# Silu as one activation for both gates of a selective-scan mixer, two elementwise steps moved from VectorE to GpSimd, and a new order of calls

## The reference, cut to what matters

```
# block 1: gated linear recurrence
x_conv = causal_depthwise_conv(x, conv_weight, conv_bias)            # 4 taps
r = sigmoid(x_conv @ Wr.T + Wr_b);  i = sigmoid(x_conv @ Wi.T + Wi_b)
a = sigmoid(log_a) ** (8 * r)
b = sqrt(clip(1 - a * a, 1e-6)) * (i * x_conv)
log_A = clip(cumsum(log(clip(a, 1e-7))), -80)                         # the limit of the decays
h = exp(log_A) * cumsum(b * exp(-log_A))
x = layernorm(x + rmsnorm(h @ out_w.T) * norm_w)
# block 2: x = layernorm(x + relu(x @ W1 + b1) @ W2 + b2)
# block 3: the mixer, with N = 16 states a channel
x_in, z = split(x @ in_proj_w.T)
x_c = silu(causal_depthwise_conv(x_in))                               # gate 1
B, C, dt = split(x_c @ x_proj_w.T);  dt = softplus(dt * dt_w + dt_b)
for t: h = exp(dt*A) * h + dt * B * x_c;  y = sum_n h * C
x = layernorm(x + (y * silu(z)) @ out_proj_w.T)                       # gate 2, the read-out of y
# block 4: x = layernorm(x + relu(x @ w1 + b1) @ w2 + b2)
```

## Time and profile before

| | |
|---|---|
| median of 3 runs | 961.75 us (959.28 to 962.03) |
| profiled execution | 961.2 us, its span 959.4 us |
| mean granted TensorE clock | 0.916 |
| busy PE / DVE / ACT / POOL | 796.9 / 802.2 / 671.6 / 561.4 us |
| instructions in the trace | 9608 |

### The profile page before, as it was taken

How to read it: one execution, slowest core, us unless ns; L and a number is a source line. 1 busy time by engine, 2 the same in 40 slices (tenths; PEclk the granted TensorE clock), 3 DMA queues, 4 the chain that set the end, 5 groups by cost and what they waited for, 6 DMA issues and landing times. The chain is left out here.

```text
span 959.4 us, 9608 instructions
## 1 busy us (share of the span) xinstructions
PE 796.9 (83%) x2802; PEld 528.2 (55%) x2802; DVE 802.2 (84%) x1013; ACT 671.6 (70%) x1345; POOL 561.4 (59%) x468
## 2 busy tenths in 40 slices
PE   2385867978987799999899999998998797787585
PEld 1264644736554556475647564756476546546464
DVE  5245566677799999999999999999999999989761
ACT  4347687588767865997699769876976685465452
POOL 0202457437836793789378937893776376565421
PEclk9597977989998889999999999999999799789597
DMA  9000000000100010001000100010000000000000
GB/s 315 12 23 22 23 1 22 1 1 0 56 1 0 1 42 13 0 1 59 8 1 1 60 1 0 1 46 0 1 1 27 1 1 1 23 0 1 22 1 22
DMA packets 10341, 19.49 MB, mean 20 GB/s; under 512 B 1457, under 2 KB 5297, under 8 KB 10289
## 3 DMA queue, kind: packets, MB, share of 16 engines
q1 hardware_dynamic: 10288, 18.88, 5.8%
HBM read 14.69 MB, written 4.19 MB: 20 GB/s over the span
## 5 line engine op out<-in xcount | busy, mean ns | idle before, releaser
L385 POOL TENSOR_TENSOR y<-y,hC 128x1024 f32<-128x1024 f32 (+3 forms) x140 | 280.1, 2001 | 77.3 <-DVE hC L1461 73.4
L1914 PE MATMUL pC<-w,hT 128*128 128x256 f32 x1024 | 232.4, 382 | 4.9 <-ACT hT L754 4.9
L819 ACT ACTIVATE dA<-dt,A_neg 128x512 f32<-128x512 f32 (+3 forms) x320 | 187.5, 630 | 54.3 <-DVE hs L1450 53.8
L1914 PEld LDWEIGHTS pC<-w,hT 128*128 128x128 f32 x1024 | 194.5, 191 | 36.7 <-issue 7.2
L1450 DVE TENSOR_TENSOR_SCAN hs<-dA,carry,pS 128x512 f32<-128x512 f32 (+3 forms) x192 | 193.4, 1008 | 18.1 <-ACT dA L819 10.4
L2037 PE MATMUL pS<-stack,sel 97*128 97x512 f32 (+3 forms) x320 | 148.0, 515 | 54.5 <-DVE hs L1450 54.0
L1435 DVE TENSOR_TENSOR pS<-u,pS 128x1024 f32<-128x1024 f32 (+3 forms) x160 | 159.8, 999 | 17.4 <-PE pS L2037 16.8
L1461 DVE TENSOR_TENSOR hC<-hs,pS 128x1024 f32<-128x1024 f32 (+3 forms) x160 | 157.5, 985 | 15.3 <-PE pS L2037 15.1
L1450 DVE TENSOR_TENSOR_SCAN hs<-dA,pS 128x512 f32<-128x512 f32 (+1 forms) x128 | 138.2, 1080 | 14.6 <-POOL carry L392 6.0
L754 ACT ACTIVATE hT<-pA,ffb_sb 128x512 f32<-128x512 f32 (+3 forms) x160 | 94.7, 599 | 59.2 <-PE pA L1907 58.9
L1907 PE MATMUL pA<-tg,w 128*128 128x512 f32 (+3 forms) x320 | 127.9, 538 | 7.7 <-ACT hT L754 6.3
(11 more groups left out here) (120 smaller groups left out, 1101.5 us busy)
## 6 DMA issues: line engine op xcount, KB each, us to landing
xt<-xT SPq DMA_DIRECT2D x6, 515.0 KB, 4.7
xtok<-x SPq DMA_DIRECT2D x6, 512.0 KB, 5.3
out<-x3b SPq DMA_DIRECT2D x6, 512.0 KB, 2.9
w<-w1a SPq DMA_DIRECT2D x1, 1024.0 KB, 8.3
w<-w2a SPq DMA_DIRECT2D x1, 1024.0 KB, 10.4
w<-w1b SPq DMA_DIRECT2D x1, 1024.0 KB, 8.3
w<-w2b SPq DMA_DIRECT2D x1, 1024.0 KB, 9.9
xt<-xT SPq DMA_DIRECT2D x2, 259.0 KB, 7.8
```

What stands on the lines that cost most here:

```text
L385: nc.gpsimd.tensor_tensor(y[:, :, 0:ch.T], so_far, hC[:, n % CRING, :, 0:ch.T], ALU.add).then_inc(S["y_sum"], 1)
L819: nc.scalar.activation(dA[:, k % ARING, 0:ch.T], dt[ch.side][:, h, 0:ch.T], ACT.Exp, scale=A_neg[:, h, n:n + 1]).then_inc(S["dA_ready"], 1)
L1914: mm = nc.tensor.matmul(dst[:, b * D:b * D + D], src(k, t0), w[:, k, :], start=k == 0, stop=k == nk - 1)
```

## The change

Both gates become one Silu activation on ScalarE; the VectorE halves and all factors 0.5 go. `decay_steps` and `readout` become GpSimd instructions. `z_silu` now waits for the read-out of the chunk two before, whose buffer it writes. Then all calls of all engines are put into another order in `opening`, `entry`, `step` and `closing`.

```
# ScalarE
-            def z_tanh(ch, h):
-                act.wait_ge(S["z_mm"], H * ch.i + h + 1)
-                nc.scalar.activation(zz[ch.side][:, h, 0:ch.T], pC[h][:, 0:ch.T], ACT.Tanh, scale=0.5).then_inc(S["tz_ready"], 1)
+            def z_silu(ch, h):
+                if ch.i > 1:
+                    act.wait_ge(S["yg_ready"], ch.i - 1)
+                act.wait_ge(S["z_mm"], H * ch.i + h + 1)
+                nc.scalar.activation(zz[ch.side][:, h, 0:ch.T], pC[h][:, 0:ch.T], ACT.Silu).then_inc(S["zz_ready"], 1)
-            def mconv_tanh(ch):
+            def mconv_silu(ch):
...
-                nc.scalar.activation(v[:, :, 0:ch.T], cv[:, :, 0:ch.T], ACT.Tanh, scale=0.5).then_inc(S["tcv_ready"], 1)
+                nc.scalar.activation(v[:, :, 0:ch.T], cv[:, :, 0:ch.T], ACT.Silu).then_inc(S["v_ready"], 1)
-                nc.scalar.mul(stack[ch.side][0:NXK, 0:ch.T], pA[0][0:NXK, 0:ch.T], 0.5).then_inc(S["stack_hi"], 1)
+                nc.scalar.copy(stack[ch.side][0:NXK, 0:ch.T], pA[0][0:NXK, 0:ch.T]).then_inc(S["stack_hi"], 1)
# VectorE
-            def z_silu(ch, h):
-                dve.wait_ge(S["tz_ready"], 2 * ch.i + h + 1)
-                V.scalar_tensor_tensor(out=zz[ch.side][:, h, 0:ch.T], in0=zz[ch.side][:, h, 0:ch.T], scalar=1.0, in1=pC[h][:, 0:ch.T],
-                                       op0=ALU.add, op1=ALU.mult).then_inc(S["zz_ready"], 1)
-            def mconv_silu(ch):
-                dve.wait_ge(S["tcv_ready"], ch.i + 1)
-                V.scalar_tensor_tensor(out=v[:, :, 0:ch.T], in0=v[:, :, 0:ch.T], scalar=1.0, in1=cv[:, :, 0:ch.T], op0=ALU.add,
-                                       op1=ALU.mult).then_inc(S["v_ready"], 1)
-                V.scalar_tensor_tensor(out=u[:, :, 0:ch.T], in0=dt[ch.side][:, :, 0:ch.T], scalar=0.5, in1=v[:, :, 0:ch.T], op0=ALU.mult,
-                                       op1=ALU.mult).then_inc(S["u_ready"], 1)
+                V.tensor_tensor(u[:, :, 0:ch.T], dt[ch.side][:, :, 0:ch.T], v[:, :, 0:ch.T], ALU.mult).then_inc(S["u_ready"], 1)
# from VectorE (dve.) to GpSimd (pool.)
+            def decay_steps(ch):
+                c = ch.i
+                pool.wait_ge(S["la_scan"], 2 * c + 2)
+                nc.gpsimd.tensor_tensor(decay[:, :, 0:ch.T], st[:, 0:H, 1:1 + ch.T], st[:, 0:H, 0:ch.T], ALU.subtract).then_inc(S["dl_ready"], 1)
+            def readout(ch, gate):
+                if gate is not None:
+                    conv_done(pool, gate)
+                pool.wait_ge(S["y_sum"], ADDS * (ch.i + 1))
+                nc.gpsimd.tensor_tensor(yg[:, :, 0:ch.T], y[:, :, 0:ch.T], zz[ch.side][:, :, 0:ch.T], ALU.mult).then_inc(S["yg_ready"], 1)
# GpSimd, one place of the new order in step()
                 if tail is not None:
                     sum_states(tail, NS - 1)
+                    readout(tail, gate)
```

More of the change, by code:

```diff
@@ L431, in entry @@
                         save_carry(scan, 1)
+                if gate is not None:
+                    decay_steps(gate)
+                if scan is not None:
+                    if scan.i > 0:
                         sum_states(scan, 1)
@@ L440, in entry @@
                         sum_states(scan, 3)
+                if prep is not None:
+                    mconv_add(prep, 1)
+                if scan is not None:
                     sum_states(scan, 4)
@@ L828, in opening @@
                     log_decay(gate)
+                if prep is not None:
+                    normalize(LN_PREP, prep, x2[prep.side])
+                if gate is not None:
                     gate_tanh(gate, 1, 0)
@@ new lines, in entry @@
+                if scan is not None:
+                    state_decay(scan, 12)
+                    state_decay(scan, 13)
+                if gate is not None:
+                    relu(0, gate, 1)
+                    relu(0, gate, 2)
+                if ahead is not None:
+                    conv_tap(ahead, 2, prep)
+                if tail is not None:
+                    row_squares(LN_OUT, tail, x3b, x3)
+                if gate is not None:
+                    relu(0, gate, 3)
+                    relu(0, gate, 4)
@@ new lines, in entry @@
+                if scan is not None:
+                    state_decay(scan, 14)
+                if gate is not None:
+                    relu(0, gate, 5)
+                if scan is not None:
+                    state_decay(scan, 15)
+                if tail is not None:
+                    normalize(LN_OUT, tail, x3b)
+                if gate is not None:
+                    relu(0, gate, 6)
+                    relu(0, gate, 7)
+                if ahead is not None:
+                    conv_tap(ahead, 3, prep)
@@ L894, in entry, with step @@
+            def step(ahead, gate, prep, scan, tail):
                 if tail is not None:
@@ L1121, in step @@
                     state_decay(scan, 12)
+                if prep is not None:
+                    step_sizes(prep)
+                if ahead is not None:
+                    conv_first(ahead)
                 if gate is not None:
@@ L1133, in step @@
                 if gate is not None:
-                    relu(0, gate, 1)
                     relu(0, gate, 2)
-                    relu(0, gate, 3)
-                if scan is not None:
-                    state_decay(scan, 15)
+                if ahead is not None:
+                    conv_tap(ahead, 2, prep)
                 if tail is not None:
@@ L1651, in entry @@
                     state_input(scan, 15)
-                if prep is not None:
-                    dt_x(prep)
-                if scan is not None:
                     state_scan(scan, 15, 0)
@@ L1669, in step @@
                     state_input(scan, 1)
+                if prep is not None:
+                    add_ffn0(prep, 0, tail)
+                if scan is not None:
                     state_scan(scan, 1, 0)
@@ L1743, in step @@
                     state_output(scan, 8)
-                if prep is not None:
-                    x_proj_low(prep)
-                if scan is not None:
                     state_scan(scan, 9, 1)
@@ L2256, in step @@
                     gate_mm(gate, 0, 1)
-                    gate_mm(gate, 1, 0)
+                if scan is not None:
+                    spread_B(scan, 3)
                 if tail is not None:
```

943 lines of the change are left out of this document (445 added, 498 removed).

## The result

The changed kernel takes 1001.5 us (median of 4 runs, 1000.8 to 1002.9), the kernel before 960.5 us beside it: a ratio of 1.043, with a 95% interval of [1.040, 1.045]. The forecast was 948.5 us.

What follows compares the result with a forecast made beforehand. VectorE was taken to bound the full steps, TensorE close behind. Gains in five stretches, less losses at start and end, summed to -12.8 us from 961.2, 948.4, left at 948.5; 8-in-10 range 934 to 965.

Steps and rivals of the forecast that it cites:

- The lengths that were kept: VectorE in a full step: four instruction groups go, 4.6 us less work, with other instructions as long as before.
- 2.5 us gained in each full step: Three full steps: each falls from 95.4 to 92.9 us, the middle of 90.9 and 95.4; -7.5 us in all.
- The step ahead of them: Stretch from 275.0 to 373.3 us: VectorE loses 4.1 us, TensorE has 14.5 to spare; taken as -3 us.
- the frame of 90.9 to 95.4: Full step length: 90.9 us if TensorE's waits are all absorbed, 95.4 if none are.
- The loads: ScalarE: 43 table loads become 80, 1.38 us each, 5.5 us a full step, 51 us in all; still below VectorE's work.
- The row that I called exp: ScalarE: a 1024-element activation of 1.06 us, used with tanh to price Silu as no change, up to 0.3 us a step.
- GpSimd's own time: GpSimd: two added steps a chunk, 4.9 us, make 73.6 us in a full step; busy near 600 us overall.
- The price that I gave, 1.2 us if the cover is gone: Results waiting behind GpSimd's moved steps: none counted in full steps, 1.2 us each if other work no longer covers them.
- The slower one, at 976 us: Rival: ScalarE sets the pace, its waits staying on top of 83.2 us of work; 0.16 together with the drain rival.

Runs made afterwards that it cites:

- e12: The changed kernel with gate input, scaled input, recurrence and u on VectorE cut to 8 columns: 962.6 us, 1.001 of the kernel before.
- e13: The kernel before with gate input, scaled input, recurrence and u on VectorE cut to 8 columns: 954.0 us, ratio 0.992.
- e8: The kernel before, old order of calls, with all helper edits but Tanh in place of each Silu, so no added loads: 953.7 us, ratio 0.992.
- e7: The changed kernel with a Tanh in place of each Silu, so no added loads: 1001.9 us against 1001.5 with them.
- e15: The changed kernel with the same four VectorE kinds cut to 8 columns and Tanh in place of each Silu: 960.1 us, 0.998 of the kernel before.
- e1: The kernel before, in its old order of calls, with only the two gates made Silu activations on ScalarE: 990.2 us, ratio 1.030.

## Why the prediction was wrong

- **The lengths that were kept.** The sum took 4.6 us a full step off VectorE and left the length of every other instruction as it was. This step failed, and it carries the most: in the full step after, recurrence, u, gate input and clip take 8.1 us more, and over the span these four groups take 42 us more. The price of it in time is about 31 of the 41 us, if the cut work of e12 and e13 is worth the same in both; how the 8.7 us that stay between e12 and e13 divide between the hold that the cut left and the new order's own chain is open. I had read the new order for loads and queues, not for what stands on GpSimd beside VectorE's instructions with two operands in SBUF. The profile of before had a sign of it. One line's instructions (min/median/max in ns), the recurrence of before:

```profile
L1388 DVE TENSOR_TENSOR_SCAN st<-decay,st,tg x20: 460/1260/3304, 29.2 to 777.1; 128x512 f32<-128x512 f32 x12, 128x256 f32<-128x256 f32 x4, 128x384 f32<-128x384 f32 x2, 128x128 f32<-128x128 f32 x2
```

  The same shape took 1.26 us and, once, 3.3 us, one instruction in 20; after the change the median of all 20 is 2.3 us.
- **2.5 us gained in each full step**, the middle between TensorE's busy time and the length of before, was mis-sized as well. In e8 VectorE has its 4.3 us less and next to nothing is held, and the three full steps take 95.5, 95.2 and 94.0 us from one scan of the logs to the next, before 95.3, 95.3 and 95.1: 1.0 us gained in place of 7.5. The step ahead of them gains 6.0 us, where 3 were forecast, so that the total of e8 is nearer to the forecast than its parts. 35 us off VectorE's busy time (e8) or 41 (e13) give 8 us of time, most of it outside the full steps. Without the hold the steps lie in the frame of 90.9 to 95.4, give or take 0.1, but at its upper end; the changed kernel's, of 100.5 to 102.4 us, lie outside it.
- **The loads.** Number (37 more), length (1283 ns) and ScalarE's busy time were right, and so was the cover in the new order: 0 us (e7), 2.5 without the hold (e15). The row that I called exp in the earlier trace rows is the logarithm of the root (L696); the exponential of it (L700) takes the same 1.06 us, so nothing hangs on it. In the old order the same loads cost 37 us; I had no number for that. The Trainium skill (ScalarE: Activation LUTs, section What ACT_TABLE_LOAD costs) adds a drain of about 1380 ns to each; the trace after shows none, 0.01 to 0.02 us between a load and its neighbours.
- **GpSimd's own time** was right (601.7 against 600). The price that I gave, 1.2 us if the cover is gone, was for what waits for GpSimd. The cost was to an engine that waits for none of its results.
- **The rivals.** The slower one, at 976 us, named ScalarE's pace. The kernel did become slower, but not by that mechanism: VectorE waits 1.0 us for dA in the full step after, and without the added loads the time is the same (e7). In the old order, which was not forecast, ScalarE's waits did stay as this rival had them: a full step of e1 takes 99.6 us with ScalarE busy for 82.9, so 16.7 us of waits are left of 17.7, and the rival has 98.2 us with 15 left. But the results that come late there are the injection, the stack and hT, and not dA.

## What to carry to other kernels

When an order is changed, list the VectorE instructions with two SBUF operands (and the tensor_scalar or copy ones from SBUF to SBUF) and look at what GpSimd runs beside each, before and after; a meeting with a GpSimd instruction of 2.4 us cost up to 2.1 us here, for a VectorE instruction of 1.2 us (u) and for one of 0.17 alike. In the trace, compare the longest with the median of one line's instructions of one shape: a factor of 2.6, as above, is a reason to look at GpSimd beside it. And where two engines are busy for 99% and 95% of a step, as here, take work off one alone and count nothing until a run shows it.
